# A fused attention and expert-layer kernel whose block ends without GpSimd's drain

## What is computed

```python
def reference(x, W_DQ, W_UQ, W_QR, W_DKV, W_UK, W_UV, W_KR, W_O, gate_w, gate_b, expert_bias, w1, b1, w2, b2):
    x = _layernorm(x + attention(x, ...))          # scores clipped to +-80, causal, softmax, @ W_O
    top = argmax(x @ gate_w.T + gate_b + expert_bias)
    out = zeros_like(x)
    for e in range(8):
        h = relu(x @ w1[e] + b1[e])                # 128 -> 512
        y = h @ w2[e] + b2[e]                      # 512 -> 128
        out = out + (top == e) * y
    return _layernorm(x + out)
```

## Time and profile before

| | us |
|---|---|
| median of the runs | 446.91 (446.22 to 447.86) |
| the profiled execution, its own time | 446.76 |
| its span, first to last instruction | 445.0 |
| TensorE busy | 414.4 (93%) |
| VectorE busy | 361.3 (81%) |
| ScalarE busy | 356.3 (80%) |
| GpSimd busy | 152.8 (34%) |
| mean granted clock of TensorE | 0.976 |

### The profile page before, as it was taken

One profiled execution on the slowest core, in us unless ns is written; L12 is line 12 of the kernel. 1 busy time (PEld: TensorE's weight loads), 2 busy tenths in 40 slices (PEclk: granted clock), 3 DMA queues, 4 the chain that ended last, 5 costly groups with the idle time before them and its releaser, 6 DMA issues. The chain is left out here.

```text
span 445.0 us, 12321 instructions
## 1 busy us (share of the span) xinstructions
PE 414.4 (93%) x4235; PEld 229.1 (51%) x4235; DVE 361.3 (81%) x824; ACT 356.3 (80%) x568; POOL 152.8 (34%) x164
## 2 busy tenths in 40 slices
PE   7899999999999999999999999998999897799970
PEld 5534344444344444434344444443345796799970
DVE  3978897999998799999888998999795586476770
ACT  3889899999988999998899999889995563466650
POOL 7221001333221112620401342240013476688882
PEclk9799999999999999999999999999999999899995
DMA  5268511478561074266202553466200456577610
GB/s 152 58 172 200 136 49 29 114 166 234 127 162 61 1 164 101 73 144 137 57 1 59 128 144 85 108 150 195 64 7 14 122 167 164 154 193 209 193 52 6
DMA packets 33005, 50.62 MB, mean 114 GB/s; under 512 B 5627, under 2 KB 16545, under 8 KB 32944
## 3 DMA queue, kind: packets, MB, share of 16 engines
q1 hardware_dynamic: 25488, 36.51, 33.7%
q10 hardware_dynamic: 5184, 9.05, 7.4%
q0 software_dynamic: 2272, 4.27, 2.9%
HBM read 21.35 MB, written 5.33 MB: 60 GB/s over the span
## 5 line engine op out<-in xcount | busy, mean ns | idle before, releaser
L1032 ACT ACTIVATE prob<-ring 128x1024 f32<-128x1024 f32 x288 | 274.5, 1040 | 25.5 <-PE ring L1224 24.6
L1242 PE MATMUL o_acc<-prob,v_stat 128*32 128x512 f32 (+3 forms) x1536 | 154.6, 497 | 2.3 <-DVE prob L705 1.4
L1224 PE MATMUL ring<-queries,keys 32*128 32x512 f32 (+3 forms) x1536 | 126.6, 384 | 0.8 <-ACT prob L1032 0.5
L1224 PEld LDWEIGHTS ring<-queries,keys 32*128 32x128 f32 x1536 | 70.5, 185 | 71.1 <-issue 45.5
L705 DVE SCALAR_TENSOR_TENSOR prob<-prob,mask_hi 128x1024 f32<-128x1024 f32 (+1 forms) x80 | 82.5, 1031 | 0.0
L691 DVE TENSOR_SCALAR prob<-prob 128x2048 f32<-128x2048 f32 x64 | 77.4, 1221 | 5.7 <-ACT prob L1032 5.3
L1120 ACT ACTIVATE prob<-ring,b1T 128x128 f32<-128x128 f32 x156 | 44.5, 368 | 37.6 <-issue 18.2
L704 DVE TENSOR_SCALAR prob<-prob 128x1024 f32<-128x1024 f32 (+1 forms) x80 | 64.4, 804 | 6.1 <-ACT prob L1032 5.4
L584 POOL DMA_INDIRECT by_expert<-xrow,index x32 | 40.8, 1276 | 78.2 <-DVE index L800 71.0
L1242 PEld LDWEIGHTS o_acc<-prob,v_stat 128*32 128x32 f32 x1536 | 33.9, 108 | 56.5 <-issue 42.1
L1365 PE MATMUL ring<-w,prob 128*128 x312 | 42.5, 280 | 6.2 <-ACT prob L1120 4.6
(11 more groups left out here) (117 smaller groups left out, 343.4 us busy)
## 6 DMA issues: line engine op xcount, KB each, us to landing
queries<-query_parts SPq DMA_DIRECT2D x60, 256.0 KB, 4.0
v_stat<-in_w ACTq DMA_DIRECT2D x34, 256.0 KB
keys<-key_parts SPq DMA_DIRECT2D x60, 128.0 KB, 2.7
queries<-by_expert SPq DMA_DIRECT2D x39, 66.0 KB
xrow<-in_x_rows SPq DMA_DIRECT2D x8, 264.0 KB, 4.4
xT<-in_x_T SPq DMA_DIRECT2D x8, 256.0 KB, 3.2
v_stat<-in_w SPq DMA_DIRECT2D x5, 256.0 KB
out<-prob,queries POOLq DMA_INDIRECT x39
```

The costliest lines, as they stand in the source:

```text
L1032: act.activation(prob[u % P_SLOTS][:, 2 * half:2 * half + 2, :].rearrange("p h s -> p (h s)"), slot(("score", u, half))[:], ACT.Exp, scale ...
L1224: last = pe.matmul(out[:, j % 2 * QC + off:j % 2 * QC + off + w], keys[hg][r, kt * P:(kt + 1) * P], queries[hg][r, qc, part, QC - w:QC], s ...
L1242: last = pe.matmul(o_acc[j * VW:(j + 1) * VW, QC - w:QC], v_stat[b % 2][:, hg, kt, j, :], prob[u % P_SLOTS][:, j, off:off + w], start=begi ...
```

## The change

One argument of the block is set. With it, the end of the block has no drain on GpSimd; the other four engines still drain, and all five meet at a barrier made of semaphores. Nothing in the engines' own functions is changed, and GpSimd's waits for the output transfers stay.

```diff
-        block = ctx.enter_context(nc.Block())
+        block = ctx.enter_context(nc.Block(no_gpsimd_drain=True))
```

## The result

| | before | after |
|---|---|---|
| median of the runs, us | 445.65 (443.19 to 447.86, 6 runs) | 438.06 (437.04 to 439.85, 6 runs) |
| ratio | | 0.9854, 95% interval 0.9826 to 0.9882 |
| the profiled execution, its own time | 446.76 | 439.83 |
| its span | 445.0 | 438.1 |
| time outside the span | 1.76 | 1.73 |

Four executions in the comparisons further down took 498 to 1260 us, where all the others took 436 to 457, and no median or ratio here counts them.

The account below looks back on a forecast made before the run. The prediction took TensorE and the tile chain to bound the body, and GpSimd's last landing, drain and barrier the end. Removing the drain's 5.86 us, with barrier and branch 0, took 446.91 to 441.05 us, range 439.8 to 442.8.

Parts of the forecast that it names:

- What bounds the end: End block: last indirect output DMA, its landing, GpSimd's branch, drain and barrier set the end; everything else ended by 435.3 us.
- Removed, 5.863 us: End block: GpSimd's one drain lies wholly on the path, so removing it gains 5.863 us if nothing takes its place.
- The last slice: Profile page's last 11.1 us: every busy row falls to nothing; no engine is busy for 6.14 us, from 438.66 to 444.80.
- The barrier, 0: Semaphore barrier replacing the one after the drain: taken as 0 us extra, bounded by -0.05 and +0.2 us.
- the branch, 0: GpSimd's branch and fetch of the end block: no fetch that the drain would hide, taken as 0 us.
- The sum: Whole kernel: median 446.91 less the drain's 5.86 gives 441.05 us, 1.3% less; span 439.1 us.
- -0.7 to +0.95: Spread allowed around 441.05 us for the level of the runs, which went from 446.22 to 447.86 us.
- If the body before 436 us has moved: Sign that would show the prediction wrong: a shift in the kernel's body ahead of the end block.
- B, the wait is handed on: After the kernel's last instruction: closing step waits instead, time outside the span grows to 7.6 us, total 446.9; chance 0.06 whole, 0.05 in part.
- C: End block: the drain stays or an instruction of the same effect replaces it, time stays 446.9 us; chance 0.03.
- D: After the barrier: closing step must stop or reset GpSimd's cores still at work, slower at 452.8 us; chance 0.02.
- What the drain waits for: GpSimd's end drain, 35 times the opening's 0.169 us: read either as real work or as nothing that holds up instructions.

Follow-up runs that it names:

- the ten drains: Changed kernel with ten GpSimd drains added in the attention stage; the four behind indirect DMAs end 3.7, 2.9, 1.5 and 1.9 us after the last such DMA's end.
- the kernel with the rest: Kernel before, with 12 VectorE operations over unused tiles that GpSimd waits for ahead of the block's end; its drain takes 5.863 us again.

## Why the prediction was right and wrong

*What bounds the end.* Right. The drain stood alone on the path, and with its removal the end follows GpSimd's last wait.

*Removed, 5.863 us.* Right, and shown both ways: gone with the drain's record, back with one hand-written drain (ratio 1.0005).

*The last slice.* One reading of the rows is wrong: GpSimd's busy row does not fall to nothing there, its last digit is 2, for its last operations. The path and the sum don't rest on it.

*The barrier, 0; the branch, 0.* Right. From the last output wait (437.7) to the end of the span (438.1) there are 0.4 us, as forecast. The new barrier has one semaphore instruction more on four engines, where they wait anyway.

*The sum.* The step that failed is the last one: "the median should come to 446.91 - 5.86 = 441.05". The difference in it is right; the base isn't. Three runs gave 446.91, six gave 445.65, and the runs of the kernel before in the four later comparisons, on four chips, lie between 441.8 and 448.4. From the new base the same subtraction gives 445.65 - 5.86 = 439.8, so the base accounts for 1.3 us of the 3.0 us by which the forecast missed. The 1.7 us that are left to 438.06 are what lies between 5.86 and the difference of the two medians, 7.6, both inside the interval of the gain, 5.3 to 7.8; no run shows a cause for them. The term that was too small was the spread of the level: "-0.7 to +0.95" was read from the highest and the lowest of three runs. On one chip the later runs of the kernel before differ by 4.1 to 5.1 us, and their medians by 2.2 us from chip to chip (444.4 to 446.6). That the three first runs had the lower clock and the other three the higher one would fit the groups by clock, but the clocks of these six are not on record. Inside the range, the parts named give 440.0 to 442.5, a tenth above the 439.9 to 442.4 that were written, which changes nothing.

*"If the body before 436 us has moved".* By this sign of its own the prediction was wrong as well: the last output DMA ends at 436.47 and not at 437.48. "The body is taken as it is" left out that two executions of one kernel differ there by as much: two profiles of the changed kernel, on two chips, have it end at 436.50 and 435.49.

*B, the wait is handed on.* Refuted: the time outside the span is 1.73 us, where it was 1.76, and lies between 1.67 and 1.90 in all runs with a drain and without. The rule drawn on from the Trainium skill, "Runtime: NRT & Kernel Launch", section "The ~15µs preamble/postamble breakdown", takes nothing from this gain: if the barrier behind the kernel waits for GpSimd, no wait is seen in the measured time.

*C and D.* Neither came. D's argument from the opening group (nothing left over from the execution before) stands; after the change the drain there takes 0.171 us, with 0.169 before.

*What the drain waits for.* Both readings missed it. It isn't work left under way, which a rest would have let end, and it isn't a wait with a fixed price. It is a debt of 0.08 us for each indirect DMA, which only a drain settles. The comparison with the opening drain was the right one, but was read as evidence on the engine ("a drain of GpSimd isn't costly in itself"), where the number of indirect DMAs ahead, none against 71, was the difference. The rule of the Trainium skill, "PSUM — Partial Sum Buffer", section "Engine vs sequencer instructions", that a drain waits until the engine is idle, agrees with the ten drains, whose records hold the operation under way, but doesn't explain the 5.9 us here: GpSimd had been idle for 11.5 us in the kernel with the rest. What the debt consists of, no run shows.

## What to carry to other kernels

Look at the records of the end block: drains and semaphore instructions count as no busy time, and the 5.9 us of the drain lay in a stretch where the page shows nothing. In this kernel a drain of GpSimd costs about 0.08 us for each indirect DMA since the last drain (other DMAs of GpSimd were not measured); if waits for the transfers already guard the output it can go, and if it must stay, an earlier drain in idle time takes over its share. Before a small difference is turned into a time, ask how well the base is known: three runs 1.6 us apart didn't show that single runs on one chip differ by 4 to 5 us.

## What had not been expected

GpSimd's drain has a price by the number of its indirect DMAs: 0.143 us for 1, 1.017 for 12, 3.892 for 47, 5.863 for 71, the same when 39 of the 71 carry 64 rows in place of 128, and 0.034 us straight after another drain.

An indirect DMA of GpSimd took longer beside long VectorE operations: the last output DMA takes 0.99 us in the kernels before and after, and 2.21 us in the one with the rest, where VectorE runs operations of 128x2048 without a pause. Half the rows change it far less: the median is 0.940 us for tiles of 64 rows and 1.034 for 128. No run here shows the cause.
